# Mixture of experts in a fused decoder kernel: every expert over every token, against tokens sorted by expert into padded segments

## The reference

```python
# H, I, E = 256, 128, 16 ; TOP_K = 4 ; x: the layer-normed tokens
logits = x.astype(jnp.float32) @ gate_w.T
scores = jax.nn.sigmoid(logits)
_, topk_idx = lax.top_k(scores + expert_bias[None, :], TOP_K)
topk_w = jnp.take_along_axis(scores, topk_idx, axis=-1)
topk_w = topk_w / jnp.sum(topk_w, axis=-1, keepdims=True)
combine = jnp.zeros((T, E)).at[jnp.arange(T)[:, None], topk_idx].set(topk_w)
def step(acc, ws):
    wg, wu, wd, cw = ws
    return (acc + cw[:, None] * _swiglu_ffn(x, wg, wu, wd), None)
routed, _ = lax.scan(step, jnp.zeros_like(x), (w_gate, w_up, w_down, combine.T))
shared = _swiglu_ffn(x, sw_gate, sw_up, sw_down)   # silu(x wg) * (x wu) wd
return routed + shared                             # x = x + tanh(g) * this
```

## Time and profile before

| | us |
|---|---|
| runs, median (lowest to highest) | 1148.67 (1143.86 to 1149.36) |
| the profiled execution | 1148.79 |
| its span in the trace | 1147.5 |
| attention 1, second half (420 to 575.8) | 155.8 |
| first experts (575.8 to 778.8) | 203.0 |
| attention 2, first sixteen steps (778.8 to 868.6) | 89.8 |
| attention 2, the rest (868.6 to 953.5) | 84.9 |

### The profile page before, as it was taken

How to read it: one execution, slowest core, us unless ns; L and a number is a source line. 1 busy time by engine, 2 the same in 40 slices (tenths; PEclk the granted TensorE clock), 3 DMA queues, 4 the chain that set the end, 5 groups by cost and what they waited for, 6 DMA issues and landing times.

```text
span 1147.5 us, 14162 instructions
## 1 busy us (share of the span) xinstructions
PE 998.4 (87%) x4772; PEld 682.6 (59%) x4772; DVE 736.2 (64%) x1792; ACT 489.6 (43%) x1174; POOL 278.6 (24%) x222
## 2 busy tenths in 40 slices
PE   5676679999999999999999999998878888976556
PEld 2222234668999998899855555655545555544444
DVE  4899993245666667766655455558857855567653
ACT  3574461137666666666611101125556542132331
POOL 2477791131111112111100011811742100010110
PEclk9787899999999999999999999999989899989677
DMA  5000001010111130110012221111000003211200
GB/s 216 0 1 0 1 0 47 0 42 29 43 42 42 42 121 29 42 42 29 1 41 70 82 61 63 56 55 43 1 1 2 1 1 133 69 42 34 74 19 18
DMA packets 16336, 46.91 MB, mean 41 GB/s; under 512 B 2300, under 2 KB 3462, under 8 KB 15624
## 3 DMA queue, kind: packets, MB, share of 16 engines
q1 hardware_dynamic: 15400, 44.67, 11.7%
q10 hardware_dynamic: 864, 1.34, 0.3%
HBM read 44.96 MB, written 1.05 MB: 40 GB/s over the span
## 4 chain that ended last, share of the span: by engine, by line
PE 68%; DVE 10%; POOL 4%; ACT 3%; issue 2%; DVEq 0%; POOLq 0%; ACTq 0%
PE psum L1442 15%; PE psum L1461 7%; PE psum L939 5%; PE psum L1131 5%; PE psum L1142 5%; PE psum L1111 5%; PE psum L800 4%; PE psum L942 3%; PE psum L1122 2%; PE psum L963 2%; PE psum L811 2%; POOL arena L1926 2%; PE psum L1697 1%; DVE arena L1731 1%; PE psum L1999 1%
## 5 line engine op out<-in xcount | busy, mean ns | idle before, releaser
L1442 PE MATMUL psum<-xT,arena 128*128 128x512 f32 x400 | 185.9, 607 | 7.6 <-DVE arena L1645 1.9
L1442 PEld LDWEIGHTS psum<-xT,arena 128*128 128x128 f32 x400 | 76.3, 194 | 86.3 <-issue 84.5
L1021 POOL TENSOR_TENSOR arena<-arena,mhalf 128x8 f32<-128x8 f32 x32 | 53.5, 1672 | 274.1 <-DVE arena L1006 274.1
L1527 DVE TENSOR_TENSOR arena<-psum,arena 128x512 f32<-128x512 f32 x50 | 34.5, 691 | 112.0 <-PE psum L1442 112.0
L1496 ACT ACTIVATE arena<-psum 128x512 f32<-128x512 f32 x50 | 29.7, 596 | 175.1 <-PE psum L1442 175.1
L1243 DVE SCALAR_TENSOR_TENSOR X<-psum,arena,X 128x256 f32<-128x256 f32 x128 | 55.9, 478 | 68.0 <-PE psum L1142 68.0
L1461 PE MATMUL psum<-arena 128*128 128x256 f32 x400 | 96.1, 382 | 2.7 <-DVE arena L1527 2.7
L1461 PEld LDWEIGHTS psum<-arena 128*128 128x128 f32 x400 | 75.8, 191 | 32.5 <-issue 21.6
L1539 DVE SCALAR_TENSOR_TENSOR X<-psum,arena,X 128x256 f32<-128x256 f32 x192 | 83.2, 478 | 9.3 <-PE psum L1461 8.9
L411 POOL TENSOR_TENSOR arena<-arena 128x512 f32<-128x512 f32 x64 | 83.5, 1331 | 7.6 <-DVE arena L728 4.8
L232 POOL TENSOR_TENSOR rstd<-rstd,mhalf 128x4 f32<-128x4 f32 x16 | 16.2, 1014 | 279.3 <-DVE rstd L225 279.2
(11 more groups left out here) (281 smaller groups left out, 1983.7 us busy)
## 6 DMA issues: line engine op xcount, KB each, us to landing
arena<-in_moe SPq DMA_DIRECT2D x50, 384.0 KB, 3.1
arena<-in_w SPq DMA_DIRECT2D x32, 384.0 KB, 3.0
arena<-in_w SPq DMA_DIRECT2D x2, 1024.0 KB, 6.0
arena<-in_gu SPq DMA_DIRECT2D x1, 1280.0 KB, 6.1
X<-in_x SPq DMA_DIRECT2D x2, 512.0 KB, 10.1
arena<-in_ctok SPq DMA_DIRECT2D x2, 512.0 KB, 6.6
arena<-in_fsideT SPq DMA_DIRECT2D x1, 1024.0 KB, 4.8
arena<-in_fside SPq DMA_DIRECT2D x1, 1024.0 KB, 7.0
```

The costliest lines, as they stand in the source:

```text
L1442: mm = nc.tensor.matmul(bank[b], m.W[:, slot, which, c * P:(c + 1) * P], k.xT[:, c, cols], start=c == 0, stop=c == DC - 1)
```

## The change

The first experts become the class `Sorted`. For each half of 512 tokens the 2048 choices (four a token) are sorted by expert and put into segments of 128 rows, each of one expert; the last segment of an expert is filled up with rows that are used by nobody. At most 31 segments are needed whatever the tokens choose, and 31 are always run.

- The head of a half, now up to 40 pieces (`sorted_head_*`): norm, router and the choice of four as before; then matmuls of the mask with triangles give every choice its rank (L1445 to L1452); small DVE operations make each expert's first segment; for each of the 31 segments one bf16 matmul of 512 columns (L1462) and one ACT operation with a sum count how many tokens come before each row, which is the row's token number. Two counts are made in a piece for half 0, beside attention 1; one in a piece for half 1, beside half 0.
- The normed tokens are written to DRAM (L1403). POOL fetches 128 of them for each segment by an indirect transfer (L1641), into a ring of six buffers for half 0, and into sixteen of their own and then the ring for half 1.
- Weights: all 16 sets are put on chip by four transfers of 1.5 MB (L1395), and the shared set by one. A segment's weights are addressed by a register, loaded from the table of segments, eight at a time (L1697).
- A segment on TensorE: two transposes of the fetched rows (L1705), two gate-and-up matmuls in which tokens stand in the array and 256 columns of weights are streamed (L1719), a transpose of the product (L1727), a down matmul of 256 columns (L1733). ACT copies the turned rows and makes the silu; DVE makes the product, copies it turned, and copies the result. SP writes the 128 results to DRAM (L1410).
- Combining: for each tile of 128 tokens POOL fetches the rows of its four choices by indirect transfers (L1907, ring of three) and DVE adds them into X, scaled (L1924): sixteen a half. Half 0's lies beside the first steps of half 1, half 1's beside the first steps of attention 2.
- Attention 2's head of half 0 starts at step 9 of half 1 of the experts; that of half 1 after the combining, with two pieces in each of attention 2's first eleven steps. In the experts' half 0, too, two pieces run in each of the first ten steps (`pieces`). Its normalised keys and queries get half the room, so that half 1 waits for the transposes of half 0.
- Many semaphores of other stages are merged into shared ones; places in SBUF move.

The core of the diff:

```diff
+class Sorted:
+    RING, BIG, YS, YG = 6, 16, 3, 3
...
+def sorted_first_sp(k, m):
...
+    for g in range(0, E, 4):
+        nc.sync.dma_start(m.W[:, g * 768:(g + 4) * 768].rearrange("p (n w) -> p n w", n=4),
+                          k.io["moe1"][g:g + 4].rearrange("n p w -> p n w")).then_inc(*k.s.landed(f"e_wall{g // 4}", tag))
...
+def sorted_sp(k, m):
+    for n in range(2 * m.NS):
+        k.sp.wait_ge(*k.s.at("e_y", m.tag, n))
+        k.nc.sync.dma_start(k.results[n // m.NS][n % m.NS * P:(n % m.NS + 1) * P, :],
+                            m.Ys[:, n % m.YS, :]).then_inc(*k.s.landed(f"e_ys{n % m.YS}", m.tag, n))
+        if n == 1:
+            sorted_tokens_sp(k, m, 1)
...
+def sorted_head_pe(k, m, h, pair, two):
...
+    for i in range(m.NS):
+        b = pair(i)[i % 2]
+        k.bank_ready(b)
+        nc.tensor.matmul(bank[b], m.oh[0:E, h, i:i + 1].broadcast_to([E, P]), m.CT[0:E, h, :],
+                         start=True, stop=True).then_inc(*tick("e_counts", tag, h, i))
+        k.free[b] = [("e_sum", tag, h, i)]
+        if i % two == two - 1:
+            yield
...
+def sorted_head_act(k, m, h, pair, two):
...
+        nc.scalar.activation(bank[b], bank[b], ACT.Sign, scale=-1.0, bias=m.rho[:, h, i:i + 1],
+                             accum_out=m.sum[:, h, i:i + 1]).then_inc(*tick("e_sum", tag, h, i))
...
+def sorted_gather_pool(k, m, n):
...
+    k.nc.gpsimd.indirect_dma_start(tile, None, k.tokens[h],
+                                   bass.IndirectOffsetOnAxis(ap=m.row[h][:, i:i + 1], axis=0)).then_inc(
+        *k.s.landed(name, tag, n))
...
+def sorted_pe(k, m, beside, times, last):
...
+    def loaded(h, g):
+
+        pe.wait_ge(*at("e_sort", tag, h, "offs"))
+        nc.tensor.load(m.regs[g % 2], m.offs[h][0:1, 8 * g:8 * g + 8])
...
+    def gate_up(n):
...
+        place = nc.tensor.snap(m.regs[i // 8 % 2][i % 8], min_val=0, max_val=(E - 1) * 768)
+        m.at_row[n] = place
+        for c in range(DC):
+            mm = nc.tensor.matmul(bank[b][:, 0:D], m.xgT[:, n % 2, c, :], m.W[:, bass.ds(place + c * D, D)],
+                                  start=c == 0, stop=c == DC - 1)
...
+    for h in range(2):
+        if h:
+            rest(beside[0])
+        first = h * NS
+        shared(h)
+        loaded(h, 0)
+        turned(first)
+        turned(first + 1)
...
+        for i in range(NS):
+            n = first + i
+            if i % 8 == 4 and i + 4 < NS:
+                loaded(h, i // 8 + 1)
+            if i + 2 < NS:
+                turned(n + 2)
+            if i + 1 < NS:
+                gate_up(n + 1)
+            elif h:
+                last()
+            if i + 1 < NS or h:
+                hidden_turned(n)
+                if i:
+                    down(n - 1)
+            for _ in range(times(h, i)):
+                step(beside[h])
...
+def combined_pool(k, m, h):
...
+    for q in range(m.Q):
+        if h or q >= m.YG:
+            pool.wait_ge(*(at("x_e", tag, h, q - m.YG) if q >= m.YG else at("x_e", tag, 0, m.Q - m.YG + q)))
+        k.nc.gpsimd.indirect_dma_start(
+            m.Yg[:, (h * m.Q + q) % m.YG, :], None, k.results[h],
+            bass.IndirectOffsetOnAxis(ap=m.rowk[h][:, q:q + 1], axis=0)).then_inc(
+            *k.s.landed(f"e_yg{(h * m.Q + q) % m.YG}", tag, h, q))
+        if q % 2:
+            yield
...
+        nc.vector.scalar_tensor_tensor(k.X[:, t, :], m.Yg[:, y, :], m.kw[:, h, q:q + 1], k.X[:, t, :],
+                                       ALU.mult, ALU.add).then_inc(*tick("x_e", tag, h, q))
...
-        step(beside[s // 16])
+        for _ in range(2 if s < 11 else 1):
+            step(beside[s // 16])
...
-    moe_pe(k, st.moe1, (moe_head_pe(k, st.moe1, 1, beside_first_experts),
-                        attention2_head_pe(k, st.attention2, 0, beside_second_experts)),
-           last=lambda: a2_scores_pe(k, st.attention2, 0))
-    attention2_pe(k, st.attention2, (attention2_head_pe(k, st.attention2, 1, beside_attention2),
+                                     later(2, sorted_head_pe(k, st.moe1, 0, beside_attention1, 2))))
+    sorted_pe(k, st.moe1, (sorted_head_pe(k, st.moe1, 1, beside_experts, 1),
+                           later(9, attention2_head_pe(k, st.attention2, 0, beside_experts))),
+              pieces, lambda: a2_scores_pe(k, st.attention2, 0))
+    attention2_pe(k, st.attention2, (later(9, attention2_head_pe(k, st.attention2, 1, beside_attention2)),
```

600 lines of the change are left out of this document (558 added, 42 removed), and 1 row of the table SHARED.

## The result

The changed kernel takes 1205.48 us, the median of four runs (1197.51 to 1207.78), against 1146.94 for the kernel before (the 1148.67 of its own table leaves out a run of 1145.21): a ratio of 1.050 [1.044, 1.056]. It is slower, as forecast, but by 58.5 us where 13 were forecast, and the time lies above the range of 1122 to 1198.

What follows compares the result with a forecast made beforehand. TensorE was taken to bound attention 1's second half and the first experts, the wait that ends last attention 2. Experts -14, attention 1 +12, attention 2 +15 made +13 on 1148.8: 1161 us, range 1122 to 1198.

Steps and rivals of the forecast that it cites:

- Expert arithmetic: First experts: 62 segments of 1.63 us; TensorE work of 138.6 us in a stage of 203.0, a gain of 64.
- Register work: First experts: 186 address instructions at 0.11 us, 20 us in all, plus eight register loads at 0.5, 4 us.
- rival A: The array sets the pace: register work hides under streaming, gathers run ahead; 1127 to 1142 us, chance 0.35.
- rival B: Register work and POOL bind: 1196 us at 0.3 per register instruction, or 1181 at 2 per gather; chance 0.15.
- Counts: Sorting's 31 bf16 matmuls a half at 0.22 us, with ranks 7.7; beside attention 1 also 3 for ACT's sums and small DVE operations.
- The weights' burst: Attention 1: four weight transfers of 1.5 MB ahead of pass 20's weights delay that pass by 1 us, from 0 to 12.
- rival C: Attention 1 waits 10 us for pass 20's weights behind the large weight transfers; 1171 us, chance 0.05.
- Who keeps up with a segment: Experts: DVE at most 1.3 and ACT 1.0 of a segment's 1.96 us, chain covered; sorting and counts cost half 0 5 us.
- POOL's chain: Attention 2's head: 26 us of powers and products stall half 1 by 11 us; attention 2 stalls 16 to 20, 8 more.
- Combining: Gathers through a ring of three cost 8 us in half 1, and 8 plus 2.5 at the start in attention 2.
- Clock: Expert stage: 2 us for a clock below 1 after stalls.

Runs made afterwards that it cites:

- f4: Changed kernel without counts, powers (multiplied instead) and combining's gathers, with DVE's result copy ahead of the pieces: 1115.43 us, 0.974 of the kernel before.
- e1: Changed kernel with segments' weights at fixed places, no register loads or address instructions: 1203.16 us, 1.050 of the kernel before.
- e13: Changed kernel with ACT's sums over half 0's counts left out, count matmuls kept, on a third chip: 1211.88 us, 1.059 of the kernel before.
- e2: Changed kernel without half 0's 31 counts (matmul and ACT's sum) beside attention 1: 1185.51 us, 1.032 of the kernel before.
- f2: Changed kernel with DVE's result copy at the end of the same step, ahead of the pieces, on a fourth chip: 1189.37 us, 1.039 of the kernel before.
- e3: Changed kernel with attention 2's eight powers on POOL replaced by products: 1176.05 us, 1.027 of the kernel before.
- e4: Changed kernel without the combining's 32 gathers, DVE adding zeros: 1184.63 us, 1.036 of the kernel before.
- f1: The changed kernel itself, unaltered, run again on a fourth chip as base: 1205.08 us, 1.050 of the kernel before.

## Why the prediction was wrong

The direction and most mechanisms were right; the sum, -14 + 12 + 15, was +1.2 + 29.1 + 21.8, less the 2.7 by which the changed kernel was ahead at 420. By its steps:

- **Expert arithmetic.** The segment of 1.63 us is exact. But f4, with every later cost out, still needs 161.5 us for the experts. Without the counts' 7.7 the prediction's arithmetic is 130.9. TensorE is busy 142.7 there and waits 18.8, 4.9 of them for gathered rows and 13.3 for DVE. Of the 142.7 the segments and the shared set are 111.4 at their price; 31.3 are left for head work, ranks and a clock of 0.95 and 0.97, where 19.5 were carried over (these weren't parted). So 41 us were in reach, not 64 plus 7.7: a base 31 too low, the largest single miss.
- **Register work.** 20 + 4 us were taken; nothing was measured (e1). So rival A was right on this cost, and rival B's price per register instruction falls: an address that is worked out ahead of a matmul did not delay it in these rows. The Trainium skill, "Runtime: NRT & Kernel Launch", section Instruction fetch mechanics, gives about 200 ns per register; here eight registers from SBUF took 0.596 us together, and with the loads left out the time stayed (e1), so its 12.8 us weren't there.
- **Counts.** The step that failed in attention 1, by its size: 0.22 us was taken from a pair of bf16 matmuls, which is right for the matmul and leaves out what its interruption of the fp32 matmuls costs, 0.24 a place, and the wait for the bank. With these it is 0.46 (e13), and with ACT's 0.12 the 31 of half 0 come to 18 us, as in e2, where 7.7 and 3 stood; those of half 1 cost 10. Another 11 in attention 1 stay without the counts; the ranks and small operations had been counted in with the 3.
- **The weights' burst** (rival C). Nothing: the pass behind it starts after 0.16 us. (The 31 us of transfers were 29 at their pace: 6144 KB against 1280 KB in 6.1.)

```profile
430.40 1.16 PE L950 MATMUL psum<-arena,cT 128*128 128x128 f32 x8 [0.16 <-DMA arena<-in_w]
```

- **Who keeps up with a segment.** This is the step that failed in kind. "Neither is full, and each result is asked for a whole segment later, so the chain through them is covered" compares busy time per segment, 1.3 of 1.96 us. Bank 5 holds one result, and the copy that frees it stood at the start of DVE's next step, behind one or two pieces of other stages. In-order waits of 26.4 us came of it, for an engine that is busy 52% of half 0 and 50% of half 1. For half 0 I had 5 us and for half 1 nothing; f2 shows 9 and 10 from the order of three lines (5 and 8 by the first profile).
- **POOL's chain.** A stall of 11 us in half 1 and one of 16 to 20 in attention 2 were forecast; TensorE waited 2.83 + 8.46 and 6.42 + 10.22 us. Cause, places and stalls are right. But from attention 2's I took off 10 us of waits that stood there before, where the row has 5.8. So 8 us of loss were 16.6 - 5.8 = 10.8 of waits and a lower clock behind them; without powers the stage is 14 us shorter (e3).
- **Combining.** 8 + 10.5 forecast (8 in half 1, 8 and 2.5 in attention 2); 9 and 10 by e4's stages. Right in size; in half 1 part of it came through DVE's queue, where the result copy stands behind the wait for a gather. The Trainium skill, "DMA: Bandwidth & Descriptors", section Anatomy of one DMA — SWDGE (gpsimd) path, gave an estimate of 2.3 us a gather; landing took 2.8 to 3.3, and POOL was held 0.95, so its variant of rival B didn't come.
- **Clock.** 2 us were set. The equal-work windows show 17 to 25, most of it inside the costs above. I had priced each wait at its length, though the kernel before already showed eight matmuls at 5.37 us for 3.60 after a wait of 1.89.

By stages the forecast fell short in the experts by 15.6 us, or by 21.5 in f1, where they take 210.1 and where the terms were read (the base 31 too low and 14 more for DVE's order, against 24 of register work that wasn't there, and that two misses offset each other here is luck); by 17 in attention 1 (7 for counts, 10 for what stays without them); and by 6.8 in attention 2 (the powers). Misses of one sign in three stages passed a range that was made for one of them at a time.

Open: why an interruption by bf16 counts costs 0.24 us (the change of type, or from 128 rows in the array to 16; around a count the weight loads stand idle 0.33 and 0.23 us), what the last 5 us or so of attention 1 are, and what the waits on the third chip are.

## What to carry to other kernels

When large matmuls are replaced by many small ones, busy shares per step no longer tell who keeps up: list, for each single buffer, what stands in the in-order queue ahead of the instruction that frees it. Price a stall at its length plus the slow stretch behind it, and price an instruction in the company it will have, not where it stands alone; what interrupts a stream is cheaper in one place than in several. An operation that nobody waited for (a power of 5.4 us on POOL) becomes the bound when its cover is what the change removes.

## What the runs showed of the hardware

- A matmul whose weights' place comes from a register runs at the pace of one with a constant place: 1.63 us a segment with both (after and e1).
- After the wait of 8.46 us the granted clock was 0.56 for the next 6.2 us, in which TensorE was full, and 1.00 after that; equal work of TensorE was busy 7 to 13% longer in f1's stages with such waits than in f2's and f4's, 3 to 10% in the first profile of the same kernel.
- An indirect transfer of 128 KB holds POOL for 0.95 us with 0.30 to the next, and lands in 2.8 (from results) or 3.3 us (from tokens).
- One bf16 matmul of 16 x 512 amid fp32 ones cost 0.46 us in half 0 and two in a row 0.68, so 0.22 each and 0.24 for the interruption; in attention 1 two cost 0.77 beside a wait for their bank.
